# The attention passes make their edges' destination logits themselves, and the set-up writes its zeros elsewhere

## What is computed

```python
h = (x @ W).reshape(num_nodes, H, C)
al_s = jnp.einsum('nhc,hc->nh', h, a_src)
al_d = jnp.einsum('nhc,hc->nh', h, a_dst)
logits = jax.nn.leaky_relu(al_s[src] + al_d[dst], 0.2)
alpha = _segment_softmax(logits, dst, num_nodes)
msg = h[src] * alpha[:, :, None]
out = jax.ops.segment_sum(msg, dst, num_segments=num_nodes)
```

## Time and profile before

| | us |
|---|---|
| median of 3 runs (8400.13 to 8410.41) | 8406.1 |
| the profiled execution | 8404.6 |
| its span, first to last instruction | 8400.0 |
| set-up and scratch zeros | 0 to 65 |
| zeroing of `support` | 65 to 136 |
| scatter loop | 136 to 1605 |
| degrees | 1605 to 1676 |
| first attention pass (its preparation before it) | 2126 to 3162 (2001 to 2125) |
| second attention pass (its preparation before it) | 3277 to 4335 (3182 to 3276) |
| four edge passes | 4335 to 8400 |

### The profile page before, as it was taken

One profiled execution on the slowest core, in us unless ns is written; L12 is line 12 of the kernel. 1 busy time (PEld: TensorE's weight loads), 2 busy tenths in 40 slices (PEclk: granted clock), 3 DMA queues, 4 the chain that ended last, 5 costly groups with the idle time before them and its releaser, 6 DMA issues. The chain is left out here.

```text
span 8400.0 us, 130868 instructions
## 1 busy us (share of the span) xinstructions
PE 6116.0 (73%) x30280; PEld 4372.8 (52%) x30280; DVE 3526.4 (42%) x13701; ACT 1570.8 (19%) x5156; POOL 5793.1 (69%) x5612
## 2 busy tenths in 40 slices
PE   2777777673788883888866666677777777777777
PEld 1444444462466651333335556566666666666665
DVE  3444444352666662555543333322222222223333
ACT  1333333221122220222212222100000000000000
POOL 3888888502677765777757777577776777767776
PEclk9888888786899995777768998778777877867776
DMA  7777777442444431111123444344443444434443
GB/s 244 114 115 115 116 114 114 73 130 70 108 115 114 115 100 20 34 34 34 35 56 117 118 117 118 94 118 117 117 117 107 118 118 117 117 105 118 117 118 107
DMA packets 503634, 871.04 MB, mean 104 GB/s; under 512 B 119784, under 2 KB 348330, under 8 KB 501098
## 3 DMA queue, kind: packets, MB, share of 16 engines
q0 software_dynamic: 331872, 673.49, 35.1%
q1 hardware_dynamic: 171658, 196.42, 7.5%
HBM read 677.39 MB, written 192.10 MB: 104 GB/s over the span
## 5 line engine op out<-in xcount | busy, mean ns | idle before, releaser
L704 PE MATMUL bank<-onehots,rows 128*128 128x128 f32 x12544 | 2526.2, 349 | 925.4 <-DMA rows<-gcn_rows,index 571.3
L648 POOL DMA_INDIRECT rows<-gcn_rows,index x2352 | 2237.5, 951 | 816.3 <-issue 657.4
L704 PEld LDWEIGHTS bank<-onehots,rows 128*128 128x128 f32 x12544 | 2076.1, 242 | 1368.2 <-DMA rows<-gcn_rows,index 732.3
L1081 POOL DMA_INDIRECT rows<-gat_rows,index x1568 | 1487.2, 948 | 587.3 <-issue 434.3
L1330 POOL DMA_INDIRECT support<-rows,index x784 | 1216.5, 1552 | 310.6 <-DMA support<-rows,index 138.6
L1162 PE MATMUL bank<-onehots,rows 128*128 128x128 f32 (+1 forms) x4704 | 995.1, 325 | 294.8 <-DVE rows L1216 293.7
L1162 PEld LDWEIGHTS bank<-onehots,rows 128*128 128x128 f32 (+1 forms) x4704 | 608.1, 186 | 700.4 <-issue 523.0
L648 POOL DMA_INDIRECT rows<-norm,index x784 | 744.3, 949 | 298.7 <-issue 224.6
L735 DVE TENSOR_SCALAR onehots<-iota,half_offset,edge_values 128x128 f32<-128x128 f32 x3136 | 855.5, 361 | 169.0 <-issue 90.5
L745 DVE TENSOR_TENSOR acc<-acc,bank 128x256 f32 x396 | 165.2, 417 | 1360.1 <-PE bank L704 1360.1
L1403 PE MATMUL cross_bank<-same_source,onehots 128*128 128x128 f32 x1568 | 374.3, 326 | 442.7 <-DVE same_source L1460 442.7
(11 more groups left out here) (263 smaller groups left out, 5877.7 us busy)
## 6 DMA issues: line engine op xcount, KB each, us to landing
source_row<-in_src_flat SPq DMA_DIRECT2D x99, 512.0 KB, 5.0
rows<-gcn_rows,index POOLq DMA_INDIRECT x2352, 2.8
support<-zeros POOLq DMA_DIRECT2D x16, 1632.0 KB, 30.2
support_rows<-support SPq DMA_DIRECT2D x40, 640.0 KB, 7.1
rows<-gat_rows,index POOLq DMA_INDIRECT x1568, 2.5
gcn_rows<-out SPq DMA_DIRECT2D x150, 128.0 KB, 1.8
own_rows<-gcn_rows SPq DMA_DIRECT2D x150, 128.0 KB
x_window<-in_x SPq DMA_DIRECT2D x98, 128.0 KB, 2.7
```

The source lines that it names most:

```text
L648: nc.gpsimd.indirect_dma_start(rows[:, k, :], None, table, bass.IndirectOffsetOnAxis(ap=index[:, k:k + 1], axis=0),).then_inc(gathered[k], 16)
L704: done = nc.tensor.matmul(by_chunk(banks[h])[:, c, :], rows[:, k, c * P:(c + 1) * P], onehots[:, k, :], start=first and c == 0, stop=final ...
L1081: nc.gpsimd.indirect_dma_start(rows[:, k, :], None, table, bass.IndirectOffsetOnAxis(ap=index[:, k:k + 1], axis=0),).then_inc(gathered[k], 16)
```

## The change

- **The destination logits in the pass.** `rows1` and `rows2` get the destination logits as further columns. In the pass, SP loads for each half the destinations of its 1024 edges onto all lanes (`dst_row`, 512 KB) and the destination logits of the 128 nodes of its window (`window_share`). DVE compares `dst_row` with the node number of each lane, which gives a one-hot matrix turned the other way for the 8 tiles (`from_window`, one buffer). PE multiplies it by `window_share`, a product of 4 columns (1 in the second step) for each tile, into PSUM (`share_bank0`, `share_bank1`), and `d` is read from there. `to_edges` and `lay_out_weights` are run only if a half's destinations span more than a window.
- **The ends.** Division, `left`, third product and what follows are done a turn later and at other places in the turn. In the second step the edge's weight is written behind its 64 scaled features, so that one product of 65 columns sums both; the sum of weights is spread before it is inverted.
- **Zeros in the set-up.** POOL issues the zeros of `support` in `set_up`, once the 12 loads have landed. The scratch zeros and the load of x go to the SP queue of the scatter stage.
- **Ends of runs by block sums.** `degrees` turns only the histogram, sums the counts of blocks by one matmul with ones and inside blocks by one with a triangle, and scans 50 columns.

```diff
 def attention_pass(...)
+                def load_half(i, n):
+                    h = n % 2
...
+                        sync.wait_ge(s.from_window_ready, i * 2 + (n - 1))
+                        sync.wait_ge(s.shared, i * 2 + (n - 1))
+                    sync.dma_start(dst_row[:, h, :], g.dst_flat[0:1, bass.ds(i * (RING * P) + n * (HALF * P), HALF * P)]
+                                   .to_broadcast([P, HALF * P])).then_inc(row_loaded[h], 16)
+                    sync.dma_start(window_share[:, h, :],
+                                   table[bass.ds(base, P), features + heads:features + 2 * heads],
+                                   allow_slow_non_contiguous=True).then_inc(share_loaded[h], 16)
...
+                def shares(i, n):
+                    h = n % 2
+                    pe.wait_ge(s.from_window_ready, i * 2 + (n + 1))
+                    pe.wait_ge(share_loaded[h], i * 16 + 16 * (n // 2 + 1))
...
+                        pe.wait_ge(s.exponent_ready, i * batches + (n - 1) * per_half)
+                    for k in range(HALF):
+                        done = nc.tensor.matmul(share_banks[h][:, k, :], from_window[:, k, :],
+                                                window_share[:, h, :], start=True, stop=True)
+                    done.then_inc(s.shared, 1)
...
                     if first:
+                        shares(i, h + 1)
...
+                        if late is not None and k == 4:
+                            ends.pe_third(pe, s, late)
                         if b is not None and k == 7:
                             ends.pe_first(pe, s, b, i * 2 + 2)
-                        if b is not None and k == 12:
+                        if b is not None and k == 13:
                             ends.pe_second(pe, s, b)
-                    if b is not None:
-                        ends.pe_third(pe, s, b)
...
+                    if inside:
+                        dve.wait_ge(s.shared, i * 2 + (batch // per_half + 1))
+                        at = batch % per_half * BATCH
+                        d = share_banks[batch // per_half][:, at:at + BATCH, :]
...
+                def turned_onehots(i, n):
+                    dve.wait_ge(row_loaded[n % 2], i * 16 + 16 * (n // 2 + 1))
+                    if not (isinstance(i, int) and 2 * i + n < 1):
+                        dve.wait_ge(s.shared, i * 2 + n)
+                    nc.vector.tensor_scalar(from_window[:].rearrange("p k e -> p (k e)"), dst_row[:, n % 2, :],
+                                            g.window_lane[:, bass.ds(i * 2 + n, 1)], None, ALU.is_equal
+                                            ).then_inc(s.from_window_ready, 1)
...
                     batch_of(i, 0)
+                    turned_onehots(i, 2)
                     add(1, base[0], i * batches + batches, i * 2 + 1)
                     if late is not None:
+                        ends.dve_divide(dve, s, late)
+                    batch_of(i, 1)
+                    if late is not None:
                         ends.dve_late(dve, s, late)
-                    batch_of(i, 1)
                     batch_of(i, 2)
+                    turned_onehots(i, 3)
+                    if late is not None:
+                        ends.dve_later(dve, s, late)
                     if b is not None:
                         ends.dve_invert(dve, s, b)
...
                     batch_of(i, 3)
-                    if b is not None:
-                        ends.dve_divide(dve, s, b)
 def scatter_by_source(...)
+                if first_pass:
+                    pool.wait_ge(g.support_zeroed, 16 * 2 * HALF)
...
+                    sync.dma_start(g.x[:], g.x_dram.rearrange("(b p) f -> p b f", p=P)).then_inc(s.kept, 16)
 def degrees(...)
+                nc.tensor.matmul(totals, ones[:], number[:], start=True, stop=True)
+                nc.tensor.matmul(after, g.earlier[:], number[:], start=True, stop=True).then_inc(s.counted, 1)
```

More of the change, by code:

```diff
@@ L967, in dve_late, with dve_later @@
     def dve_late(self, dve, s, b):
+        pass
+    def dve_later(self, dve, s, b):
         pass
@@ L1898, in _, with attend, lay_out_shares @@
                 link(nc.vector.tensor_copy(g.narrow_range[:], flags[:, 2:3]))
-def attend(nc, g, table, logits, features, heads, segment, scratch, planes, kind, again, before, **fields):
+def attend(nc, g, table, logits, features, heads, segment, scratch, planes, kind, inside, again, before, **fields):
+    def lay_out_shares():
+        with ExitStack() as stack:
+            sbuf, _ = tiles_of(stack, nc)
+            a_dst = sbuf("a_dst", [P, g.blocks, heads])
+            spread = sbuf("spread", [P, g.tiles, heads])
+            filled = sbuf("filled", [P, g.tiles, heads])
+            with phase(nc) as (block, s):
+                @block.vector
+                def _(dve):
+                    nc.vector.tensor_copy(a_dst[:], g.self_logits[:, :, heads:2 * heads])
+            to_edges(nc, g, a_dst, heads, scratch[heads], spread, filled)
+            lay_out_weights(nc, g, filled, None, spread, heads, planes)
     attention_bound(nc, g, heads)
```

348 lines of the change are left out of this document (212 added, 136 removed).

## The result

The changed kernel takes 8427.1 us (median of 20 runs, 8406.1 to 8458.9) against 8406.2 (20 runs, 8399.8 to 8410.4): ratio 1.0026, 95% interval 1.0016 to 1.0036. It is slower by 0.26%, 21 us. The forecast was 8460, 54 us slower, in a range of 8300 to 8620: the sign and the range held, the loss was put more than twice too high. The profiled execution is one of the slower ones: 8439.5 us, its span 8434.4, which is 34.4 more than that of before. The runs of the changed kernel spread over 53 us, those of the kernel before over 11.

What follows compares the result with a forecast made beforehand. POOL's gathers were taken to bound the passes, with little PE slack. From 8404.6 us, -241 ahead of the passes, +243 in pass one and +51 in pass two gave 8457.6, with 1.5 stated as 8460; range 8300 to 8620.

Steps and rivals of the forecast that it cites:

- What bounds the passes: Attention passes: POOL's gathers set 20.02 us a turn; PE has 2.3 us of slack, not in one piece.
- What is taken off: Ahead of the passes: zeros -10, degrees -31, preparations -120.5 and -91.5 us.
- T: DVE's comparison of 1024 elements a lane, twice a turn: 0.75 us, bounds 0.65 and 1.2.
- The cycle: Full-clock turn: DVE's wait for PE's products stalls PE 1.7 and 0.9 us; 23.7 us against 20.03.
- The clock: PE in pass one: one low stretch of 3.5 us a turn adds 1.3, so 25.0, between 23.7 and 28.
- Pass one: First attention pass: 49 turns, each 4.97 us longer, +243 us.
- Pass two: Second attention pass: 21.5 us a turn, 1.05 over 20.45, as waits lower the clock; +51 us.
- The sum: Whole kernel: 8404.6 less 241, plus 243 and 51, is 8457.6; with 1.5, 8460 us.
- The clock holds: Rival, both passes: 23.7 us a turn in pass one, POOL's 20.03 in pass two; 8324 us, chance 0.27.
- Low most of the time: Rival, clock in both passes: 28 and 23.8 us a turn; 8719 us, chance 0.12.
- The products nearly free: Rival, both passes: waits covered, small products' loads hidden, POOL's 20.03 us a turn; 8144 us, chance 0.06.
- the change does what it says: Opposed rival, whole kernel: part of the -241 stays away, for instance zeros still waited for; 8480 to 8700 us, chance 0.05.

Runs made afterwards that it cites:

- short comparison: Changed kernel with DVE's comparison covering 128 elements in place of 1024: 8269.6 us, ratio 0.9840 to the kernel before.
- filler: Changed kernel with extra identity products on PE in the stalls of pass one, into unused columns: 8383.5 us, ratio 0.9970 to the kernel before.
- later comparison: Changed kernel with DVE's comparisons moved behind a turn's second and fourth batches, from behind the first and third: 8181.5 us, ratio 0.9735 to the kernel before.
- one share product: Changed kernel with one share product a half, read by all eight tiles: 8212.1 us, ratio 0.9776 to the kernel before.
- spread products: Later comparison plus two buffers, with share products two by two behind a half's first four tiles: 8176.8 us, ratio 0.9728 to the kernel before.
- two buffers: Changed kernel with two `from_window` buffers, comparison's place kept: 9608.1 and 9609.7 us on slow chips, ratios 0.9835 and 0.9831 to the kernel before.
- last version: Spread products plus sums cleared while a pass's first destinations load: 8168.1, 8173.1 and 8204.1 us, ratio 0.9742 to the kernel before.

## Why the prediction was right or wrong

**What bounds the passes** was read rightly: POOL, with PE's slack too small for the new products. 20.03 was measured again where pass one comes from the preparation.

**What is taken off** held: preparations within 0.3 us; zeros -9.4 for -10, which is luck, since the -10 was a choice between -20 and nothing; degrees -36.0 for -31. The turnings brought 21.3 for 20.5, the new operations cost 1.6 for 3, and the stage begins 2.8 us sooner behind the last scatter, which I hadn't counted.

**T** was 0.75 as scaled from the cast, and its place in the cycle is shown by the short comparison. The eight shares took 1.71 for 1.65.

**The cycle** was right piece by piece: middle of the turn 5.48 us (2718.05 to 2723.53) for 5.57, stall 1.63 for 1.7; start of the turn 4.77 (2706.13 to 2710.90) for 4.74, stall 0.90 for 0.9. The largest miss is the fourth batch with the spreading, 4.23 (2700.19 to 2704.42) for 4.44. The 0.22 from PE's end to DVE is a misreading: the rows give 0.25 (2617.66 to 2617.91), and here it is 0.29 counted from the next product's start. The pieces as listed add up to 23.6 and not 23.7. The turn is 23.34 for 23.7: 0.36 x 47 = 17 us of the miss.

**The clock** is the step that I could only size by a choice, "one low stretch of 3.5 us a turn": +1.3 for a turn. The mean turn is 24.46, 1.10 above the median of 23.36: +1.1. That the two are close is luck, since the kind was wrong. What costs are stretches of 14 us at the low clock, as at 2452, each beginning at a stall of 1.6 us (the one at 2452 ends at 2453.27 after 1.57) and worth 6 us of the turn, in every third turn of a good part of the pass (the turn behind it is 1.0 us shorter); the short ones come beside. The filler showed that it is the stalls that bring them, and the small products that I had held against the clock didn't hurt it in the later comparison (0.99). 0.2 x 47 = 10 us of the miss.

**Pass one** as a whole is the step that failed. The mechanism was right, the term "the first pass +49 x 4.97 = +243" was too large: 47 turns of 4.43 more make +208. Of these 35 us 17 are the cycle, 10 the clock, and the rest, some 8, comes of counting 49 turns, two of which stand in the first turn and the tail. With those two it is +227; the tail of +9.0 I had at zero.

**Pass two** missed the other way, +51 for +66.5, 21.5 for 21.82 a turn. The reason given, waits that bring down the clock, holds only in part: the clock fell to 0.54, but the later comparison has 0.53 and 20.39 a turn. The turn also falls to 20.40 with the short comparison and to 20.46 with one share product. What costs there is the wait with T and the products in the cycle, not the low clock by itself.

**The sum** misses the profiled execution by 19 us (+53 for +34), and this one is 12 us above the median of its 20 runs. Both together make 54 into 23; the other 2 or so are that the kernel before has its profiled execution 1.5 us below its median, and that 8457.6 and 1.5 are 8459.1, not 8460. How many long low stretches a run has varies, which I take for the spread of 8406 to 8459 us; the granted clocks of the runs (0.792 in the fastest, 0.785 in the slowest) agree with it by and large (one run of 8427.6 also has 0.792), but no second profile shows it.

**The rivals.** "The clock holds" didn't come: 0.92 in pass one and 0.54 in pass two. With the filler it held in pass one (0.98), and the time was 8383.5 and not 8324, above all since pass two stayed at 21.75 a turn where that rival has 20.03. "Low most of the time" is far from 0.92. "The products nearly free" is refuted by the single share product and by the spread products. The Trainium skill's sentence on the weight loads that are pulled ahead ("TensorE: Matmul & The Clock Gate", section "Architectural detail: the array is 16× 32×32, not 1× 128×128") doesn't help here: these loads cost 0.107 to 0.117 us each wherever they stand, 0.11 being also what a load with 128 columns of product takes in the earlier trace rows. That the change does what it says is seen in the table.

## What to carry to other kernels

A single buffer between two engines costs little as such; what costs is the work that stands behind the wait on the waiting engine, if it is what the other engine needs next. Put such an operation where its condition has long been met: here it moved past one batch, and the same work went from 24.5 to 20.9 us a turn. Where a stall can't be avoided, look at what the clock does behind it, which costs on top: here 1.1 us a turn to the 2.5 us of the stalls. Four tenths of a microsecond off each stall ended the long low stretches.

## What the runs showed of the hardware that I had not expected

Products into unused columns made the kernel 43 us faster, by keeping the clock.

Three of five chips took 16% longer for the kernel before, all runs alike, and the order of the versions is another there. The filler and the short comparison were 2.7 to 3.6% slower than the kernel before, though they lie below it at 8400; the later comparison and the two buffers were 1.6 and 1.7% faster, one share product 2.2%, and the last version, 2.6% faster at 8400, only 0.3 to 0.5%. The granted clock is lower too: 0.73 for the later comparison against 0.80. In the traces there an engine starts late though all that it waits for is shown as done. In the second run of the short comparison (kernel before at 9706) PE has finished its eight shares at 2698.77, where the half's first product starts, and DVE's comparison begins 5.2 us later; in the changed kernel above it is 0.29 us:

```profile
2698.77 0.69 PE L1259 MATMUL bank<-onehots,rows 128*128 128x128 f32 x4
```

```profile
2704.00 0.29 DVE L1318 TENSOR_SCALAR from_window<-dst_row,window_lane 128x128 f32<-128x128 int32 x1 [8.95 <-DMA support<-rows,index]
```

```profile
2704.08 0.34 SPq L1145 DMA_DIRECT2D dst_row<-in_dst_flat  x1
```

The releaser named there belongs to another stage. What came late is PE's count. SP's next load, the last of the three rows, waits for the same semaphore `shared` and starts at the same moment, and the trace's record of semaphore updates has `shared` counted up at 2703.86. In pass one of that trace 46 of the 97 recorded counts come more than 1 us behind the end shown for the last share product, most of them 4.9 us; in the changed kernel's trace all 98 come within 0.02. Whether the products themselves end late there or only their count arrives late can't be told, since the ends of products are modelled. The scatter loop has the pace of the other chips, the attention and edge passes don't. Why some chips do this stays open.
